# A graph attention kernel: at most two gathers of a group under way, with two semaphores a buffer

## The reference, cut to what matters

```python
Q = (enh @ Wq + bq).reshape(N, H, D); K = ...; V = ...      # N = 6250 nodes, H = 4 heads, D = 64
mod_k = K[src] + 0.2 * rel_w[edge_relations][:, None, :]    # 200000 edges, sorted by dst
scores = jnp.einsum('ehd,ehd->eh', Q[dst], mod_k) / D ** 0.5
w = softmax of scores over the edges of each dst
agg = jax.ops.segment_sum(w[:, :, None] * V[src], dst, num_segments=N)
```

## Time and profile before

| | us |
|---|---|
| median of 3 runs, not profiled | 3118.36 |
| profiled execution, first to last instruction (span) | 3766.5 |
| of it: up to the first gather | 127 |
| of it: six groups of gathers into free buffers, then waiting | 69 |
| of it: the gathers of the other 255 groups | 2487 |
| of it: the last groups of the edge pass | 34 |
| of it: `finish` | 1049 |

### The profile page before, as it was taken

One profiled execution on the slowest core, in us unless ns is written; L12 is line 12 of the kernel. 1 busy time (PEld: TensorE's weight loads), 2 busy tenths in 40 slices (PEclk: granted clock), 3 DMA queues, 4 the chain that ended last, 5 costly groups with the idle time before them and its releaser, 6 DMA issues. The chain is left out here.

```text
span 3766.5 us, 76572 instructions
## 1 busy us (share of the span) xinstructions
PE 3074.1 (82%) x21228; PEld 2157.6 (57%) x21228; DVE 1702.1 (45%) x6065; ACT 1484.9 (39%) x4653; POOL 1958.4 (52%) x2036
## 2 busy tenths in 40 slices
PE   8687777778778777778778777777777998999998
PEld 6454444444444444444444444444446888889898
DVE  6244444444444444444444444444476654563222
ACT  5343333333333333333333333333335554554332
POOL 6346556555556556555555555555345444432322
PEclk9798888888888888888888888888858999999999
DMA  7556666676666666666666666666475666666764
GB/s 221 167 158 189 192 188 187 186 192 190 186 188 190 191 187 188 188 191 191 185 186 192 190 186 190 189 192 190 129 229 165 207 192 193 191 185 174 199 183 133
DMA packets 292075, 701.47 MB, mean 186 GB/s; under 512 B 44040, under 2 KB 139679, under 8 KB 291796
## 3 DMA queue, kind: packets, MB, share of 16 engines
q0 software_dynamic: 151888, 456.15, 44.2%
q1 hardware_dynamic: 140036, 243.55, 21.4%
HBM read 633.18 MB, written 66.36 MB: 186 GB/s over the span
## 5 line engine op out<-in xcount | busy, mean ns | idle before, releaser
L257 POOL DMA_INDIRECT e_kv<-d_kv,idx x1566 | 1493.8, 954 | 1115.9 <-PE psA L533 660.7
L533 PE MATMUL psA<-e_kv,e_probT 128*32 128x128 f32 x6264 | 518.5, 285 | 297.9 <-issue 292.5
L417 DVE TENSOR_REDUCE e_small<-psD 128x1 f32<-128x384 f32 x261 | 145.4, 557 | 1213.2 <-remote 1209.7
L496 PE MATMUL psK<-consts,e_kv 128*128 128x128 f32 x3132 | 606.7, 327 | 14.7 <-issue 12.6
L317 ACT ACTIVATE e_carried<-psA,e_small 128x130 f32<-128x130 f32 x261 | 96.4, 369 | 1106.5 <-PE psA L533 1101.8
L533 PEld LDWEIGHTS psA<-e_kv,e_probT 128*32 128x32 f32 x6264 | 200.6, 108 | 527.1 <-issue 493.6
L496 PEld LDWEIGHTS psK<-consts,e_kv 128*128 128x128 f32 x3132 | 429.1, 166 | 127.1 <-issue 121.1
L2034 PE MATMUL f_psY<-f_w,f_hT 128*128 x1680 | 397.3, 390 | 44.1 <-ACT f_hT L1626 28.1
L1558 POOL DMA_INDIRECT out<-f_y,f_whose x105 | 166.6, 1587 | 469.1 <-DVE f_y L1892 298.1
L2021 PE MATMUL f_psH<-f_xT,f_w 128*128 128x128 f32 x3360 | 402.4, 279 | 0.0
L1626 ACT ACTIVATE f_hT<-f_psH,f_b 128x128 f32<-128x128 f32 x840 | 236.9, 371 | 413.7 <-PE f_psH L2021 336.5
(11 more groups left out here) (292 smaller groups left out, 4309.4 us busy)
## 6 DMA issues: line engine op xcount, KB each, us to landing
f_w<-in_W SPq DMA_DIRECT2D x113, 1024.0 KB
e_rows<-d_feat SPq DMA_DIRECT2D x174, 288.0 KB
e_kv<-d_kv,idx POOLq DMA_INDIRECT x1566
d_accs<-e_accs SPq DMA_DIRECT2D x87, 195.0 KB
f_xs<-d_xs SPq DMA_DIRECT2D x105, 132.5 KB
d_kv<-p_kv SPq DMA_DIRECT2D x48, 256.0 KB, 2.1
p_x<-in_x SPq DMA_DIRECT2D x49, 128.0 KB, 2.7
n_v<-d_kv SPq DMA_DIRECT2D x49, 128.0 KB
```

The source lines that it names most:

```text
L257: pool.indirect_dma_start(out=kv[g.slot][:, t, :], out_offset=None, in_=kv_dram[:, :], in_offset=bass.IndirectOffsetOnAxis(ap=idx[g.slot][ ...
L496: mm = pe.transpose(psK[:, half, t * P:(t + 1) * P], kv[a.slot][:, third * TS + t, half * P:(half + 1) * P], ident)
L533: mm = pe.matmul(psA[own, 0:2 * HD], probT[c.slot % R][:, j, own], kv[c.slot][:, s * TS + j, D + b * P:D + (b + 1) * P], start=j == 0, sto ...
```

## The change

GpSimd waits, before gather t of a group (t from 2 to 5), for the landing of gather t - 2 of the same group. So that this can be told, each buffer gets two semaphores, one for the even and one for the odd gathers, and PE and ACT wait for both. The first two gathers of a group wait for no landing.

```diff
 RING = 6
+FLIGHT = 2
+KVS = 16 * TG // FLIGHT
...
-    s_kv = [sem(f"es_kv{i}") for i in range(U)]
+    s_kv = [[sem(f"es_kv{i}_{j}") for j in range(FLIGHT)] for i in range(U)]
...
                     for t in range(TG):
+                        landed = s_kv[g.slot][t % FLIGHT]
+                        if t >= FLIGHT:
+                            hold(pool, landed, g.rnd * KVS + t // FLIGHT * 16)
                         pool.indirect_dma_start(
                             out=kv[g.slot][:, t, :], out_offset=None, in_=kv_dram[:, :],
                             in_offset=bass.IndirectOffsetOnAxis(ap=idx[g.slot][:, t:t + 1], axis=0),
-                        ).then_inc(s_kv[g.slot], 16)
+                        ).then_inc(landed, 16)
...
-                    act.wait_ge(s_kv[n.slot], n.rnd * (16 * TG))
+                    for landed in s_kv[n.slot]:
+                        act.wait_ge(landed, n.rnd * KVS)
...
-                    pe.wait_ge(s_kv[a.slot], (a.rnd + 1) * (16 * TG))
+                    for landed in s_kv[a.slot]:
+                        pe.wait_ge(landed, (a.rnd + 1) * KVS)
```

## The result

The changed kernel takes 4395.24 us (median of 4 runs, 4393.22 to 4406.16) against 3116.82 us before (4 runs, 3114.65 to 3118.64): a ratio of 1.4108 [1.4092, 1.4125], +1278 us. The forecast was slower by 15% (3575 us, 3190 to 3900): right in direction, short by 820 us, and the result lies above its range. To read what follows: the kernel before takes 3115 to 3118 us in some sessions (this result and the last two experiments; mean granted clock 0.935) and 3763 to 3822 us in the others (0.87), all its runs in a session alike, profiled or not, and chip 7 showed both, 3811 and 3117; the changed kernel takes 4395 to 4458 us beside either.

What follows compares the result with a forecast made beforehand. It took POOL, at or very near its own rate of 7.5 us a group, as the bound. With 9.3 after the change, 1.8 x 255 = 459 us on 3118.4 gave 3577, rounded to 3575 us; range 3190 to 3900.

Steps and rivals of the forecast that it cites:

- the chain: POOL's waits for landings in the edge pass: group time T = 2.5 + 2(L + w), 9.7 us by profiled durations.
- L: Time from the start of a gather to its landing, taken as 3.1 us.
- w: Time from a landing to the start of the next gather on POOL, taken as 0.5 us.
- The shrink from 9.7 to 9.3: Group time in timed runs taken as 9.3 us, as recording was expected to stretch descriptor work and landings little.
- rival E: Gathers in the edge pass queue behind SP's row loads and POOL waits out each delay: 3909 or 4062 us; chance 0.15.
- Parts (2) to (4): Edge pass: lateness barely buffered (30 us in all); extra PE and ACT waits taken as 0; bytes, addresses and packets unchanged.
- The ring: Six-deep buffers of the edge pass let POOL run ahead once, by at most some 4 groups, 30 us in all.
- A: Faster: two gathers in flight hold PE's `psA` and the maximum less; 3067 or 2914 us; chance 0.10.
- B: No change: timed group at 8.1 us, landings shrink to T = 8.0; 3118 within 6 us; chance 0.05.
- C: Slower by little: T = 8.0 to 8.6 over 7.5, or 8.7 over 8.1; 3246 to 3400 us; chance 0.20.
- F: POOL's waits are met at once and compute is the bound: 3118 us; chance 0.02.
- D: The forecast itself: group time between 8.7 and 10.2 us in the timed runs, 3400 to 3800 us; chance 0.48.

Runs made afterwards that it cites:

- the last two experiments: Changed kernel with never more than two gathers under way, also across groups: 4600.23 us; then the kernel before, unchanged, profiled: 3116.82 us.
- the strict form: Changed kernel with gathers 0 and 1 also waiting for gathers 4 and 5 of the group before: 4600.23 us, 1.4753 of the kernel before.
- the half-size runs: Gathers cut to 1 KB rows after the first six groups: kernel before 3816.73 against 3821.8 us, changed kernel 3970.82 against 4458.14 us.
- runs of three: Kernel before with gather 3 waiting for gather 0, and gather 0 for gather 3 of the group before: 3924.51 us, 1.0271.

## Why the prediction fell short

**The base was right.** "I take 7.5 us a group in the timed runs", POOL at its own rate: 7.58 measured. The reason given, that recording might stretch the profiled execution, was wrong: profiled executions take what the others take. The error of this step is 0.1 x 260 = 20 us.

**The form of the chain was right, its terms too small.** With the L + w = 4.15 of the quiet group shown, the same chain gives 2.5 + 2 x 4.15 = 10.8 for the change (11.02 in that group), 1.25 + 5 x 4.15 = 22.0 with one gather under way (22.78, loads within) and 3 x 4.15 = 12.45 for the strict form (12.23 in a stretch without a load).

**The step that failed is the price of a landing**: L + w was put at 3.6, and the two steps of a group are 4.38 and 4.27 us even where no load falls into it. A second step failed too: the row loads were left out of the sum. By terms, from 9.3 to 12.47:

- L was taken as 3.1, under the 3.3 and 3.7 of the loads of POOL's queue, with the argument that fewer gathers are queued ahead. The median is 3.6: +1.0 a group. With one under way, or two strictly, it is still 3.4, so there was hardly a queue to be relieved of. The nearest rows said 3.3 and 3.7, and the value was put under them for a reason that no row bore.
- w was taken as 0.5, between 0.30 and 0.78. It is 0.74: +0.5.
- The shrink from 9.7 to 9.3, for timed runs quicker than profiled ones, is not there (span 4392.1, own time 4393.98): +0.4.
- The row loads and stores of sums stood in rival E, not in the sum. Every third group takes 14.66 instead of 11.37: +1.1. Without the loads a group is 0.8 shorter, shown by its own run; that the other 0.3 are the stores is likely, not shown. A mechanism that is there in every third group by the counts of the earlier trace rows is a term, not a rival.
- The chain let gather 5 follow gather 4 after 1.25 us. It waits for gather 3, so from gather 4 to the next group it is 2.73 and not 2.5, without a load: +0.2.

Together that is 3.2, which is the gap. In all 12.47 - 7.58 = 4.89 over 1565 / 6 groups is the 1276 us of the stretch.

The Trainium skill ("DMA: Bandwidth & Descriptors", section on the anatomy of one DMA) would have made L 2.6 and the sum 306 us; the trace has 3.6. By the half-size runs an estimate is that 1.2 to 1.4 of it are the bytes, for which the page gives 0.6, and some 2.2 don't depend on them, for which it gives 2.0. Its row on HBM latency says that a lighter load shortens the fixed part; the medians go that way, 3.4 against 3.6 us, while the shortest landing is 3.2 in both, so the trace neither confirms nor excludes it.

**Parts (2) to (4).** The ring hid nothing of a lower rate, as said. The second semaphore costs PE and ACT next to nothing: 1.0012. "In the profiled execution its span hardly moves" was wrong: against the kernel before of the same session, where that takes 3811 or 3822 us, the change costs 619 to 636 us, since T was taken as 9.7 and is 12.3 to 12.5.

**The rivals.** A's mechanism is real where the kernel before takes 3.8 ms: what PE has done reaches ACT and DVE late while gathers run, and with gathers in pairs it no longer does (no "remote" wait is left for the maximum in the changed kernel's profile of such a session). But it saves far less than the chain costs: L + w would have to be under 2.5 and is never under 3.96 in groups 8 to 249 of the changed kernel. B, C and F are excluded by 12.47, and so is the forecast's own bracket (D, 8.7 to 10.2). E was the nearest, and its mechanism held. It priced a group with a load at 12.5, 2.8 above the plain one; measured are 14.66 and 3.3. So the extra was priced about right, on a plain group that was 1.7 too short.

**What stays open.** Why, where the kernel before takes 3.8 ms, the releases from PE come some 1.0 to 1.6 us after the end of POOL's last issue. It isn't the bytes (half of them: 0.9987), nor the row loads (0.9966), nor the density of issues at 0.3 to 0.5 us of pause (0.997, 0.9944). It goes with the number of gathers (1.35 us each), and survives runs of three and of six behind a landing. Why the same program has these two times was not found either. Nor was any form but the change and the strict one timed beside the base of 3117.

## What to carry to other kernels

A limit on the transfers under way trades a rate for a latency: with k under way one can start every (L + w) / k at best, so set that against the engine's own issue interval first; here 4.15 / 2 = 2.1 stood against 1.25, and a wait four places back (4.15 / 4 = 1.04) cost almost nothing (1.009, where POOL also waited for `psA`). Take L from the nearest transfer on the same queue, add what shares the DMA engines as a term of its own, and expect an engine that waits for single landings to pay for its neighbours' traffic (210 us here), which one that only issues hardly feels (10 us). Profile the kernel before in the session in which it is timed; here a profile 21% longer than the runs was not the cost of recording.

## What the runs showed of the hardware

- A gather of 128 rows of 2 KB takes 3.2 us at least from its start to its landing, 3.6 in the median, up to 7.6 (the changed kernel's profile); the next one that waited for it starts 0.74 us after the landing.
- POOL's issues of such gathers never came closer than 1.24 us (0.94 and 0.30), and where they followed each other without a wait the DMA engines moved 242 GB/s at a share of 0.86.
- Four more waits a group on POOL, if already met, leave its gathers 1.25 us apart.
- The granted clock of the gather stretch is 0.78 in the changed kernel and 0.93 in the kernel before at 3117 us: PE is busy in 63% and 83% of it. Since PE waits 1078 us for rows there, I take the low clock as a consequence and not a cause; no run tested it.
